# Shifted copies and scaled tables moved from VectorE to ScalarE, and an addition moved ahead of the first scores, in a two-layer decoder kernel

## The reference, cut to what matters

```
for i in range(DEPTH):                                     # 6 layers
    x = attn_layer(shift_tokens(x), Wqkv[i], q_scale[i], k_scale[i], Wo[i]) + x
    x = ffn_layer(shift_tokens(x), ln_g[i], ln_b[i], W1[i], b1[i], W2[i], b2[i]) + x

shift_tokens(t): features 0..63 stay, features 64..127 come from the token before (0 for the first)
attn_layer: qkv = x @ Wqkv; 16 heads of 64; q = l2norm(q) * qs; k = l2norm(k) * ks
            q = q*cos*scale + rotate_half(q)*sin*scale;  k the same with 1/scale
            softmax(8 * q k^T) over a window of 32 tokens and the one before it; out = attn @ v; out @ Wo
ffn_layer:  layer norm (g, b), W1 to 682 columns, a * gelu(gate), @ W2 + b2
```

## Time and profile before

| | |
|---|---|
| median of three runs | 1828.43 us (1827.32 to 1828.60) |
| the profiled execution, its own time | 1826.93 us |
| its span in the profile | 1825.0 us |
| stage F's first and last addition of the attention's output (L683), twelve in all | start at 950.1 and 1797.7 us |
| busy in the whole span: PE, DVE, ACT, POOL | 1598.0, 1211.4, 904.7, 583.9 us |

### The profile page before, as it was taken

The page is one execution under the profiler, slowest core; times in us unless marked ns, Lnnn a source line. Parts: engine busy times, 40 slices in busy tenths (PEclk is TensorE's granted clock), DMA queues, the critical chain, the costliest instruction groups (busy, mean ns, idle before and its releaser), DMA issues.

```text
span 1825.0 us, 37900 instructions
## 1 busy us (share of the span) xinstructions
PE 1598.0 (88%) x15445; PEld 865.5 (47%) x15445; DVE 1211.4 (66%) x2060; ACT 904.7 (50%) x1581; POOL 583.9 (32%) x546
## 2 busy tenths in 40 slices
PE   7877656999999998676899999999999999989996
PEld 2545324556556654221364454545546454453543
DVE  6685566556656564433777776877867787687773
ACT  2445322453444343223566566666666656656563
POOL 5461000000000000000556455465544646545461
PEclk9998567999999999677899999999999999999998
DMA  7130010000000000002313313142231422314120
GB/s 244 36 98 1 0 30 11 7 20 1 21 20 1 21 1 1 1 1 89 124 43 120 106 44 121 63 125 84 77 124 37 148 76 75 109 52 136 57 82 12
DMA packets 49514, 110.48 MB, mean 61 GB/s; under 512 B 15168, under 2 KB 20032, under 8 KB 48192
## 3 DMA queue, kind: packets, MB, share of 16 engines
q1 hardware_dynamic: 49344, 108.07, 18.2%
HBM read 28.61 MB, written 0.52 MB: 16 GB/s over the span
## 4 chain that ended last, share of the span: by engine, by line
PE 53%; DVE 27%; ACT 9%; issue 5%; DMA 2%; POOL 2%; SPq 1%; DVEq 0%; ACTq 0%
DVE nm L652 4%; PE ps L285 4%; PE ps L290 4%; DVE nm L638 3%; PE ps L1506 3%; PE ps L423 3%; PE ps L413 3%; PE ps L274 3%; PE ps L1557 3%; DVE big L655 2%; PE ps L1566 2%; PE ps L1525 2%; PE ps L396 2%; DMA big<-big 2%; DVE big L1750 2%
## 5 line engine op out<-in xcount | busy, mean ns | idle before, releaser
L699 POOL TENSOR_TENSOR big<-big 128x512 f32<-128x512 f32 x112 | 142.9, 1276 | 903.3 <-DMA big<-big 902.4
L708 POOL TENSOR_TENSOR big<-big,nm 128x384 f32<-128x384 f32 x224 | 189.4, 866 | 186.7 <-DVE nm L645 186.7
L603 DVE TENSOR_TENSOR big<-ps,big 128x512 f32<-128x512 f32 x224 | 153.7, 686 | 84.4 <-ACT sq L485 56.1
L538 ACT ACTIVATE big<-big 128x384 f32<-128x384 f32 x224 | 109.4, 522 | 126.1 <-DVE big L655 125.9
L604 DVE TENSOR_TENSOR big<-ps,big 128x512 f32<-128x512 f32 x224 | 152.6, 681 | 0.0
L413 PE MATMUL ps<-big 128*64 128x64 f32 x3584 | 129.1, 225 | 24.1 <-ACT big L550 23.8
L413 PEld LDWEIGHTS ps<-big 128*64 128x64 f32 x3584 | 115.1, 138 | 64.6 <-ACT big L550 47.5
L1750 DVE TENSOR_TENSOR big<-ps,fix 128x512 f32<-128x512 f32 x192 | 119.2, 683 | 36.4 <-PE ps L1506 36.0
L700 POOL TENSOR_TENSOR big<-big 128x512 f32<-128x512 f32 x112 | 143.1, 1277 | 0.0
L396 PE MATMUL ps<-ident,big 128*128 128x128 f32 x896 | 128.5, 282 | 14.5 <-POOL big L708 12.5
L692 POOL TENSOR_TENSOR big<-big 128x512 f32<-128x512 f32 x84 | 107.1, 1275 | 72.2 <-ACT big L530 72.1
(11 more groups left out here) (286 smaller groups left out, 2892.3 us busy)
## 6 DMA issues: line engine op xcount, KB each, us to landing
big<-big SPq DMA_DIRECT2D x224, 256.0 KB, 2.4
big<-big SPq DMA_DIRECT2D x112, 128.0 KB, 2.4
big<-in_F_w SPq DMA_DIRECT2D x6, 1536.0 KB, 6.7
big<-big SPq DMA_DIRECT2D x84, 64.0 KB, 2.0
big<-in_D_w SPq DMA_DIRECT2D x12, 256.0 KB, 2.9
big<-in_F_wo SPq DMA_DIRECT2D x6, 512.0 KB, 4.4
big<-in_F_w SPq DMA_DIRECT2D x6, 341.0 KB, 3.0
big<-in_A_w SPq DMA_DIRECT2D x1, 1536.0 KB, 11.1
```

The costliest lines, as they stand in the source:

```text
L603: dve.tensor_tensor(tmp[:, i, w, :], ps[:, k, :], tb[:, 2 * w, :], ALU.mult).then_inc(*part.mark((key, b, p, 0)))
L708: pool.tensor_tensor(v, v, nm[:, p % 3, 16 + 4 * h:20 + 4 * h].unsqueeze(2).to_broadcast([128, 4, KW]), ALU.mult)\
```

## The change

Three pieces of DVE's work in the steps are moved. The shifted copy of late[3] goes to ACT's late[3], as two ACTIVATEs with Copy. The four multiplications of the tables go to ACT, two behind step 4 and two behind step 5, as ACTIVATEs with Copy and a per-partition scale; DVE gets a wait for them at the first rotation of a layer, and ACT two waits in front of them. The first layer's tables stay on DVE with a signal of their own. The feed-forward's addition stays on DVE and goes from late[1] to a place behind a_parts_dve and ahead of the first maxima.

```
         def a_rope_dve(dve, key, b, p, l2):
             i, n = slot(b, p), NP * b + p - 3
+            if l2 and n == -3 and key[1] > 0:
+                dve.wait_ge(*tab_made.at((key[1], 1)))
...
                     a_parts_dve(dve, key, b)
+                if "down" in early:
+                    early["down"]()
                 for p in range(NP):
                     a_top_dve(dve, key, b, p)
...
+        def f_move_act(act, l, b):
+            act.wait_ge(*x_new.at(("Ff", l, b)))
+            step(act, act_step, act.activation(xsh[0:64, b, :], x[0:64, cols(b)], ACT.Copy))
+            act.activation(xsh[64:128, b, 1:T], x[64:128, T * b:T * b + T - 1], ACT.Copy).then_inc(moved, 1)
+
+        def f_tab_act(act, l, i):
+            act.wait_ge(scl_in, 16 * (l + 1))
+            act.wait_ge(*k_part.at((("F", l - 1), B - 1, NP - 1, 1)))
+            for j in (2 * i, 2 * i + 1):
+                ins = act.activation(tab[:, j, :], tab0[:, j, :], ACT.Copy, scale=scl[:, i:i + 1])
+            ins.then_inc(*tab_made.mark((l, i)))
...
+            l, late = key[1], {3: lambda: f_move_act(act, *u)}
+            if b == B - 1 and l + 1 < LAYERS:
+                late[4], late[5] = lambda: f_tab_act(act, l + 1, 0), lambda: f_tab_act(act, l + 1, 1)
...
-            ins.then_inc(*tab_made.mark(l))
-            dve.wait_ge(*tab_made.at(l))
+            ins.then_inc(*tab_first.mark(l))
+            dve.wait_ge(*tab_first.at(l))
...
-            def move():
-                dve.wait_ge(*x_new.at(("Ff", *u)))
-                shift_dve(dve, u[1], (moved, 1))
             if u is not None:
-                early = {4: lambda: f_scale_dve(dve, *u), 6: lambda: f_mul_dve(dve, *u, 0), 7: multiply}
-                late[1], late[3] = lambda: f_add_dve(dve, *u), move
-            if b == B - 1 and l + 1 < LAYERS:
-                late[5] = lambda: f_tab_dve(dve, l + 1)
+                early = {4: lambda: f_scale_dve(dve, *u), 6: lambda: f_mul_dve(dve, *u, 0), 7: multiply,
+                         "down": lambda: f_add_dve(dve, *u)}
...
-                    sp.wait_ge(*tab_made.at(l))
+                    sp.wait_ge(*(tab_made.at((l, 1)) if l else tab_first.at(0)))
                     f_w_sp(sp, l + 1)
```

More of the change, by code:

```diff
@@ L1869, in build @@
         f_const, scl_in, ff_in_ = raw("f_const"), raw("scl_in"), raw("ff_in_")
-        tab_made = sg("tab_made")
+        tab_made, tab_first = sg("tab_made"), sg("tab_first")
         F_FF = 5 * 16
@@ L1971, in f_act_hooks @@
             return ({3: lambda: f_square_act(act, *u), 4: lambda: f_root_act(act, *u), 5: lambda: f_xn_act(act, *u), 6: lambda: f_gelu_act(act, *u, 0),
-                     7: lambda: f_gelu_act(act, *u, 1), "up": last}, {})
+                     7: lambda: f_gelu_act(act, *u, 1), "up": last}, late)
         def f_act(act):
```

## The result

The changed kernel takes 1811.02 us in the median (1810.78 to 1811.41, four runs) beside 1827.88 for the kernel before in its four runs: a ratio of 0.991, with a 95% interval of 0.9893 to 0.9927. That is 16.9 us faster; I had predicted 14.6 and a time of 1813.8. By the interval the gain lies between 13.3 and 19.6 us. The profiled execution spans 1808.9 us in place of 1825.0, 16.1 less.

What follows compares the result with a forecast made beforehand. PE was taken as the bound, held up by DVE at some points. Six passes gaining 0.78 us and five gaining 1.98 made 14.6, so 1812.3 against the profiled execution and 1813.8 as median; range 1808.1 (rounded down) to 1822.5, chance 0.85.

Steps and rivals of the forecast that it cites:

- The bound: Stage F's steps: PE sets a step without extra DVE work; extra work makes DVE late and holds PE up.
- The rival that DVE's relief counts in full: All work taken off DVE counts, 1.85 us a pass and 2.8 for the tables: 34.4 us, 1794.0; chance 0.03.
- The addition: DVE, moved ahead of the first maxima: these 0.37 us late, 0.85 saved at the old place, 0.50 gained a pass.
- Step 1's row sum: DVE in step 1: 0.35 us late, because ACT's copy of v and then its exponentials are late.
- Step 2's maxima: DVE at step 2: start at 1378.33 instead of 1378.83, 0.5 us earlier.
- The mask of step 3: PE at step 3, had waited 0.46 us for DVE's subtraction; put at 1380.80, 0.13 us earlier.
- The values in step 3: PE in step 3, had waited 0.25 us for ACT's copies; gain 0.50 us, kept to the mask of step 4.
- The copy: Shifted copy off DVE behind step 3: relieves 1.37 us, gains PE 0.28 a pass; two ACTIVATEs on ACT cost 0.
- the values of step 5: PE in step 5: 0.21 us wait through ACT's chain plus 0.07 restart goes, 0.28 us a pass.
- The tables: Four multiplications, 2.8 us on DVE: moving them gains 1.20 us in each of five passes; cost on ACT 0.
- the two windows: First maxima to the next pass's first rotation: 39.40 us with tables, 38.20 without; the difference is 1.20 a pass.
- The 0.57 and 0.67: PE's waits in us, in passes with tables, after DVE's four multiplications; predicted to be gone.

Runs made afterwards that it cites:

- the filled kernel: Changed kernel plus one needless 128x512 copy on DVE behind each of steps 4, 5 and 6; 1809.84 us beside 1825.07 for the kernel before.
- the two experiments: Kernel before with only the addition moved, 1820.49 us; changed kernel with the addition back at its old place behind step 1, 1816.87 us.
- copy back: Changed kernel with the shifted copy back on DVE behind step 3; 1813.89 us beside 1824.87 for the kernel before.

## Why the prediction was right, point by point

**The bound.** PE sets steps 4 to 6, as said; the filled kernel shows it. The rival that DVE's relief counts in full (34.4 us) is out: the eleven passes gave 15.1. With it goes, here, the reading that the prediction took from the Trainium skill, Perfetto Trace Analysis, section "Identifying the Most-Contended Engine", which names the engine by occupancy and judges TensorE by MFU (its arithmetic as a share of the peak) and the share of weight loads. By the latter VectorE came first, and still 14 us of VectorE work could be put back for nothing. MFU was not worked out here.

**The addition.** First maxima 0.37 late foreseen, 0.40 measured. Step 0's row sum unmoved: it follows the first maxima by 3.15 us, before by 3.55, so with the 0.40 it is at the same time. Step 1's row sum late by the same 0.4, which the 0.38 in front of it for ACT shows; with the addition one place further up there is no such wait, and it is in time. Step 2's maxima 0.50 early foreseen, 0.46 measured. The mask of step 3 gained 0.14 (0.13 foreseen): it follows the first maxima by 10.66 + 0.40 for 11.20. The values in step 3 and the mask of step 4 gained 0.50 and 0.51 (0.50 foreseen). Worth 0.50 a pass by the working, 0.53 and 0.51 in the passes with tables of the two experiments.

**The copy.** 0.28 us foreseen through the values of step 5; the mask of step 6 follows at 23.69 + 0.40 for 24.87, 0.78 in all, as foreseen. On ACT the two copies took 0.624 and 0.626 us for 0.629, and were hidden. Alone it was worth that only in passes without tables; the prediction never said so, and its sum was right because the tables went as well.

**The tables.** 1.20 foreseen from the two windows, 1.29 measured. The two windows began at the first maxima; the whole of a pass with tables is 77.5 as the others are, since the projections behind a pass without tables are about 1.3 us shorter. The pair on ACT took 1.34 us as foreseen and left no wait in front of step 5's exponentials, where 0.4 had been reckoned at most. The 0.57 and 0.67 of the earlier trace rows and the wait of step 7's mask are gone, and the steps of both kinds, cut as in the earlier trace rows, take 37.0 us from first maxima that are 0.40 late, the 37.4 foreseen.

**The sum.** Six passes at 0.78 and five at 1.98 made 14.6; the passes of the profile gave 15.1. The differences are the tables' 0.1 five times and 0.3 in the last pass, which has no next unit to overlap with, less a little in the passes without tables. Two things that the forecast put at nothing came out otherwise in the profile: the tail behind the last pass, 1.4 us shorter by the clock, and the time ahead of the first addition, 0.4 longer. With them the profile has its 16.1. The medians' 16.9 is a further 0.8, for which no run shows a cause; the timed runs have no profile, so how long their tails were is not shown either. The changed kernel's second job, 1811.16 beside 1825.07, gives 13.9. The median's gain thus moves by 3 us from one job to the next, and the 2.8 us between 1813.8 and 1811.02 lie within that. What confirms the working is the passes.

## What to carry to other kernels

Where engines take turns at the bound, an operation is worth not its duration but what its absence lets the next engine start earlier; here 1.37, 0.85 and 2.8 us of VectorE work were worth 0.28, 0.5 and 1.3 us a pass, and that could be read beforehand by following each wait's releaser through the steps. A relief ahead of a later hold-up on the same engine can be worth nothing until that one is gone too, so a single edit can measure as zero and count when made together with others, as the copy did. And look for the wait just in front of the place where work is put: one place further up, ahead of q's norm, the same addition was free, another 4.2 us in the eleven passes.

## What the runs showed of the hardware

The last feed-forward's tail runs with gaps on PE, of 1.80 and 3.21 us among others, and partly at the lower clock level. With the same instructions it took 27.30 us at a mean granted clock of 0.72, 25.90 at 0.76 and 24.60 at 0.87, and the last two are the same kernel. A pair of matmuls that took 1.13 us at 1.00 took 2.08 at the lower level. A difference of one or two microseconds between single profiles of this kernel can come from there, and once (copy back) the last pass was slowed too. That is why lengths of passes, which repeated to 0.01 us in those with tables, told the parts apart better than medians did.

Copies on ACT from SBUF took 0.624 us for 64x512 and 0.626 for 64x511 that start at partition 64 and write at an offset of one element, beside 0.629 for the 128x512 of L514: neither the start partition nor the offset, which the prediction had feared, cost anything that shows.
